# Products that nobody reads, put where TensorE waits, at five places of a two-layer graph network kernel

## What is computed

```python
def layer0(h, w, a, src, dst):
    hi, hj = h[src], h[dst]
    e = leaky_relu(concat([hi, hj]) @ w, 0.2) @ a
    att = exp(e) / segment_sum(exp(e), src)[src]
    return segment_sum(hi * att, dst)

def layer1(x, src, tgt, W, A_left, A_right, residual):
    H = x @ W                                   # 4 heads of 32
    s = exp(leaky_relu(H_s[src] + H_t[tgt]))    # scaled by the maximum
    alpha = s / (segment_sum(s, src)[src] + 1e-8)
    return elu(segment_sum(alpha * H[tgt], src) + x @ residual)

x = layernorm(x + layer0(x, w, a, src, dst))
x = layernorm(x + layer1(x, src, dst, ...))
```

## Time and profile before

| | us |
|---|---|
| median of 3 runs | 3270.96 |
| lowest and highest | 3270.72 and 3272.41 |
| time of the profiled execution | 3272.64 |
| its span, first to last instruction | 3270.8 |
| TensorE busy | 3043.9 (93%) |
| VectorE busy | 3046.4 (93%) |
| ScalarE busy | 2749.3 (84%) |
| mean granted clock of TensorE | 0.974 |

### The profile page before, as it was taken

One profiled execution on the slowest core, in us unless ns is written; L12 is line 12 of the kernel. 1 busy time (PEld: TensorE's weight loads), 2 busy tenths in 40 slices (PEclk: granted clock), 3 DMA queues, 4 the chain that ended last, 5 costly groups with the idle time before them and its releaser, 6 DMA issues. The chain is left out here.

```text
span 3270.8 us, 101515 instructions
## 1 busy us (share of the span) xinstructions
PE 3043.9 (93%) x40072; PEld 2778.1 (85%) x40072; DVE 3046.4 (93%) x4921; ACT 2749.3 (84%) x6951; POOL 155.3 (5%) x251
## 2 busy tenths in 40 slices
PE   5777699999999998899999999988999999999995
PEld 4666577777778776899999999988999999999993
DVE  8999889999999998899999999978999999999996
ACT  6988888888888886899999999976888888888886
POOL 0000000000000000000000000000111111111110
PEclk9899899999999999899999999998999999999998
DMA  2000022222222222233333333315444444444441
GB/s 66 13 14 11 22 99 92 88 93 94 91 89 93 94 86 59 74 96 96 97 97 96 97 97 96 96 47 177 164 161 164 161 164 161 164 161 163 162 137 41
DMA packets 173823, 333.06 MB, mean 102 GB/s; under 512 B 54876, under 2 KB 109616, under 8 KB 173264
## 3 DMA queue, kind: packets, MB, share of 16 engines
q1 hardware_dynamic: 170996, 323.30, 30.9%
q10 hardware_dynamic: 2348, 3.20, 0.3%
HBM read 320.77 MB, written 5.66 MB: 100 GB/s over the span
## 5 line engine op out<-in xcount | busy, mean ns | idle before, releaser
L1009 PE MATMUL l_gathered<-xp,l_src_onehot 128*128 128x128 bf16 x7203 | 467.1, 221 | 11.2 <-DVE l_src_onehot L922 11.2
L1420 PE MATMUL l_gathered<-hp,l_onehot 128*128 128x128 bf16 x7203 | 459.3, 219 | 0.0
L704 PE MATMUL sc_z<-sc_onehot,pq 128*128 128x256 f32 (+1 forms) x2450 | 419.7, 293 | 23.3 <-DVE sc_leaky L617 18.3
L1009 PEld LDWEIGHTS l_gathered<-xp,l_src_onehot 128*128 128x128 bf16 x7203 | 407.9, 99 | 26.4 <-DVE l_src_onehot L922 11.7
L847 DVE TENSOR_TENSOR l_lane<-iota_b,l_lane_pairs 128x896 bf16<-128x896 bf16 x686 | 421.9, 615 | 0.0
L617 DVE SCALAR_TENSOR_TENSOR sc_leaky<-sc_z,sc_leaky 128x1024 f32<-128x1024 f32 (+3 forms) x325 | 370.7, 1141 | 52.8 <-ACT sc_leaky L788 45.3
L788 ACT ACTIVATE sc_leaky<-sc_z 128x1024 f32<-128x1024 f32 (+3 forms) x325 | 309.4, 952 | 124.3 <-PE sc_z L708 121.4
L1420 PEld LDWEIGHTS l_gathered<-hp,l_onehot 128*128 128x128 bf16 x7203 | 406.9, 98 | 0.4
L708 PE MATMUL sc_z<-sc_onehot,pq 128*128 128x256 f32 (+1 forms) x2450 | 394.2, 282 | 0.0
L1434 PE MATMUL l_acc<-e,l_lane_wide 128*128 128x132 f32 x2744 | 386.0, 284 | 0.3 <-ACT e L1498 0.3
L704 PEld LDWEIGHTS sc_z<-sc_onehot,pq 128*128 128x128 f32 x2450 | 334.6, 191 | 35.5 <-issue 34.1
(11 more groups left out here) (242 smaller groups left out, 6108.2 us busy)
## 6 DMA issues: line engine op xcount, KB each, us to landing
rows_got<-edge_rows_wide SPq DMA_DIRECT2D x343, 448.0 KB, 3.6
l_got<-edge_rows_src SPq DMA_DIRECT2D x343, 224.0 KB, 3.1
placed<-edge_rows SPq DMA_DIRECT2D x144, 512.0 KB, 3.6
out_dram<-X SPq DMA_DIRECT2D x12, 256.0 KB
edge_rows<-e SPq DMA_DIRECT2D x98, 6.1 KB
edge_rows_wide<-e SPq DMA_DIRECT2D x98, 12.2 KB
sc_last_rows<-edge_rows SPq DMA_DIRECT2D x24, 64.0 KB, 3.6
placed<-edge_rows SPq DMA_DIRECT2D x6, 256.0 KB, 3.8
```

Source lines behind the costliest of these rows:

```text
L704: nc.tensor.matmul(z[:, b, 0:nw, :], PQ[:, b0 + b, q, 0:C], hot[:, r % HOTS, b, 0, 0:nw, :], start=(b == u and q == 0), stop=False)
L1009: ins = nc.tensor.matmul(gps[:, t % 2, i * P:(i + 1) * P], hot[:, t % RING, i, :], parts[:, g * GX + i, q, :], start=(q == 0), stop=(q == 2))
L1420: ins = nc.tensor.matmul(gps[:, t % 2, i * P:(i + 1) * P], dst_hot[:, t % RING, i, :], hp[:, g * GX + i, q, 0:C], start=(q == 0), stop=(q ...
```

## The change

A helper `keep_warm` issues products of the identity with a row of numbers that is in SBUF anyway: 512 columns in bf16 (384 in one place), into a PSUM bank whose content nobody needs at that time. Its products are put on TensorE's stream at five places: in the last two passes of binning (8 at each of three points), ahead of the first step of the scores (6), between the last denominator sums of the scores (one of 384 columns after each of the last eleven groups of `add`, 6 after the last `turn`, 3 at the very end), ahead of the first layer's first gather (24), and in that layer's first steps (4 after each of the first seven gathers, 4 between the two parts of each of the first seven `add_up`). Two waits are added, on work that has long been done when they are reached: on the last copy of `base`, and on DVE's last but one leaky relu, so that the bank may be overwritten. No other engine's stream changes.

```diff
@@ bin_windows @@
-        base_ps = ps("base", [P, 512])[:, 0:NB]
+        base_bank = ps("base", [P, 512])
+        base_ps = base_bank[:, 0:NB]
@@ TensorE's loop of bin_windows @@
                     if 0 <= n < NB:
                         take_off(n)
+                    if n == NB - 1:
+                        pe.wait_ge(s["base_summed"], NB)
+                        keep_warm(nc, k, base_bank, 8)
                     if 0 <= n + 1 < NB:
                         rank(n + 1)
                     if n >= 1:
                         turn(n - 1)
+                    if n >= NB - 1:
+                        keep_warm(nc, k, base_bank, 8)
                     if 0 <= n + 1 < NB:
                         project(n + 1)
@@ score_edges @@
+                keep_warm(nc, k, nps, 6)
                 pe.wait_ge(s["const"], 1)
                 for r in range(LAST + 1):
                     if r < R:
                         gather(r)
+                    if r == R + 1:
+                        pe.wait_ge(s["leaky"], R - 1)
...
                     for pair, i in items_due(r - 1):
                         add(pair, i)
+                        if r > R:
+                            keep_warm(nc, k, zps[:, (R - 2) % 2], 1, 3)
                     for pair in due("turn", r):
                         turn(pair)
+                        if r > R:
+                            keep_warm(nc, k, zps[:, (R - 2) % 2], 6)
                 nc.tensor.matmul(nps[:, 0:3 * NB], k.ident_b[:], zeros[:], start=False, stop=True).then_inc(s["closed"], 1)
+                keep_warm(nc, k, zps[:, (R - 2) % 2], 3)
@@ new @@
+def keep_warm(nc, k, bank, times, runs=4):
+    for _ in range(times):
+        nc.tensor.matmul(bank[:, 0:runs * P].rearrange("p (u l) -> p u l", l=P), k.ident_b[:],
+                         k.iota_b[:].unsqueeze(1).to_broadcast([P, runs, P]), start=True, stop=True)
@@ layer0_sums @@
+        unread = ps("unread", [P, 512])
@@ add_up(t), between its three products and its four @@
+                    if t < PER:
+                        keep_warm(nc, k, unread, 4)
                     pe.wait_ge(s["low"], t + 1)
@@ TensorE's loop of layer0_sums @@
+                keep_warm(nc, k, unread, 24)
                 for t in range(-1, R):
                     if t + 1 < R:
                         gather(t + 1)
+                    if t + 1 < PER:
+                        keep_warm(nc, k, unread, 4)
                     if t >= 0:
                         add_up(t)
```

## The result

The change makes the kernel slower: 3290.59 us median of 22 runs, against 3271.02 of 22 runs of the kernel before. The medians are 0.6% apart; over all runs, of which 9 of 22 are much lower than that median, the ratio is 1.0037 (95% interval 1.0025 to 1.0049). That is outside the forecast's range of 3269.5 to 3275.0.

What follows compares the result with a forecast made beforehand. The prediction took DVE and ACT to set the first layer's pace, TensorE slightly ahead, and few waits for TensorE elsewhere. Terms −1.06, −0.39, +0.5 and +2.4 gave +1.45 on 3270.96, so 3272.4 us, range 3269.5 to 3275.0.

Steps and rivals of the forecast that it cites:

- sum of +1.45: All places together: −1.06 − 0.39 + 0.5 + 2.4 us, added to 3270.96 for a forecast of 3272.4 us.
- Terms 1 and 2: End of binning and start of the scores: faster work and removed waits would win 1.06 and 0.39 us.
- the last rival: First layer: clock changes differ between executions; won-back low-clock time at gather(6) and gather(7) gives 3269 to 3270 us; chance 0.06.
- the slower rival: First layer: unread products don't raise the clock, steps 5 and 6 lose 5.8 + 4.1 us, time 3282; chance 0.03.
- Binning, −1.06: End of binning: the clock holds, fill(48) takes 1.79 instead of 2.77 us and turn(48) 0.26 instead of 0.34.
- Start of the scores, −0.39: Start of the scores: ACT's two waits for TensorE, 0.21 and 0.18 us, go.
- End of the scores, +0.5: End of the scores: unread products delay turn and the closing product by 0.17 us each and outlive the reduction by 0.2.
- the rival's low-clock case: End of the scores: if the clock is low there, the cost is +1.4 us; the edges' rival, 3274.4, had chance 0.12.
- Hidden products of the first layer, 0: First layer, 24 products ahead and steps 0 to 4: they fit in TensorE's idle time and cost 0 us.
- Exposed products, +2.4: First layer, steps 5 and 6: twelve products ahead of gather(8) push DVE and ACT back 2.4 us, kept to the stage's end.
- The price: One unread bf16 product of 512 columns on TensorE was taken to cost 0.225 us, with bounds of 0.124 and 0.43.

Runs made afterwards that it cites:

- e1: The whole change run again without edit; 4 of 12 runs at 3291.2 to 3292.5 us, median of the others 3273.6, against 3270.9 for the kernel before.
- e4: The change cut to its products at the end of binning and ahead of the scores; all six runs at 3286.9 to 3289.7 us.
- e6: e4 with four more clearings of a tile on DVE at the scores' start; 11 runs at 3270.6 to 3274.1 us, kernel before 3272.4.
- e3: The change cut to its products at the end of the scores; median 3272.8 us, against 3270.9 for the kernel before.
- e8: Whole change without the first layer's twelve exposed products and the scores' end, plus three products in pair 23's closing wait; 3273.1 us, ratio 1.0003 to before.
- e12: Whole change plus three unread products in TensorE's wait at the end of the scores' pair 23; median 3273.8 us, ratio 1.0001 to the kernel before.
- e9 to e11: Kernel before with four, five and six more DVE clearings at the scores' start; medians without the runs above 3286 us: 3273.9, 3273.5, 3274.2, against 3272.4.

## Why the prediction was wrong

The mechanisms of the five places mostly held, and their sum of +1.45 is 0.6 us from what the lower group lost in the first measurement and 1.3 in e1. That it came so near is in part luck: the end of the scores cost more than its term, the first layer less. The step that failed is the one that comes before them: I looked only at the five places of the change and took every us won at one of them as won at the end. Terms 1 and 2 were written as −1.06 and −0.39 and nothing else; that an earlier end of binning also moves 850 us of scores in time was not considered. The falls cost 18.5 us in half of the runs. In the terms of the prediction: −1.06 − 0.39 was taken as the whole effect of these two places, and with them alone (e4) all six runs are some 18 us above the kernel before. The thought was near: the last rival says that the clock's changes fall differently in each execution, but I used it only for the first layer, only as a gain, and gave it 0.06. And the slower rival had the right kind of mechanism, TensorE held at the low clock while it is needed, in the wrong stage, with 0.03.

Point by point:

- *Binning, −1.06.* Right: 1.78 and 0.26 us, and 1.07 us by the first one-hot. In the profiles the scores' first one-hot starts at 403.8 to 405.5 where these products are in (405.0 with e6's clearings), and at 405.7 and 405.9 where they aren't.
- *Start of the scores, −0.39.* Right: ACT's waits are gone, and from the first one-hot to the wait at the end of pair 22 it takes 819.17 us (403.96 to 1223.13) instead of 819.76 (405.70 to 1225.46), −0.6 in these two profiles.
- *End of the scores, +0.5.* Right where the clock stays high (+0.4 in e1's profile); where it falls, +1.4 to +1.8, the rival's low-clock case and a little more, and +1.9 in e3's median. The short products keep the clock up in some runs and not in others.
- *Hidden products of the first layer, 0.* Right: e8's stage is as long as before's.
- *Exposed products, +2.4.* Mechanism right, size 1.7 to 1.8. The price was right (0.217 against 0.225), and 2.1 us were lost by the first sum; that it is kept to the end was not: 0.3 to 0.4 us came back over the stage. The Trainium skill's 131 ns for such a product (TensorE: Matmul & The Clock Gate, Back-to-back issue gap) does not fit the trace; its figure for an isolated one, some 216 ns, does.
- *Sum, +1.45.* The lower runs are 2.1 us (first measurement) and 2.8 us (e1) over before; the end of the scores would account for the difference where the clock is low there, but the lower runs have one profile each, one with it low and one with it high.

What would have found it: the windows over the whole of the scores, with the question where TensorE's stream gets light, rather than only where it is idle, and above all where it stays light afterwards, as in the last pair.

## What to carry to other kernels

Where an engine's clock follows its load, list the places where its stream gets thin while others depend on it, outside the edited code too: a saving of one or two us anywhere ahead moves those places in time and can tip them. Look first for a thin stretch with lighter work behind it; 21 such waits in front of full-width work did nothing here. A short wait is cheaply filled: with three products in one of 0.67 us, 0 of 12 runs are in the upper group, where 17 of 34 were in earlier sets of runs. And a product that nobody reads is free only in a real wait: where the next work is already due, each cost 0.2 us, in the end 0.15. And with so few as three runs such a kernel can show either group; look at all runs before a median, and at the clock beside each.

## What the runs showed of the hardware

- TensorE can be at the low level while it is busy without a break: 44.5 of 44.5 us in e4 from 1260.5 us, nearly all of it steps of half the usual width. The same stream at the high level keeps it (21.98 of 22.00 us busy at 1.00 in e12). So in these profiles the last pair holds the level that it starts with.
- A fall came without a long idle time: the longest wait in the last 35 us ahead of the fall in e4 was 0.66 us. The Trainium skill (TensorE: Matmul & The Clock Gate, Why this matters for your kernels) warns of idle gaps between bursts; this stream has none of that kind, only thin work around a short wait.
- Where the clock's changes fall against the program isn't the same in each run, but not spread evenly either: 2 of 119 runs of the kernel before are upper, and 6 of 6 of e4. The kernel before ran on all the chips and e4 on one only, and 1, 6 and 2 of 12 runs are upper with delays of 1.4, 1.8 and 2.2 us (e9 to e11) on a single chip. Why the moments keep such a relation to the program stays open.
